# Experts' attention on one Trainium2 core: the transposes of the normalised average, the values' projection and the output's projection each placed one step later

## The reference, cut to what matters

```python
def expert_step(acc, params):
    qw, qb_, kw, kb_, vw, vb_, ow, ob_, g = params
    q = (x @ qw.T + qb_).reshape(B, S, H, Dh).transpose(0, 2, 1, 3)
    k = (x @ kw.T + kb_).reshape(B, S, H, Dh).transpose(0, 2, 1, 3)
    v = (x @ vw.T + vb_).reshape(B, S, H, Dh).transpose(0, 2, 1, 3)
    scores = jnp.einsum('bhqd,bhkd->bhqk', q, k) * scale
    p = jax.nn.softmax(scores, axis=-1)
    o = jnp.einsum('bhqk,bhkd->bhqd', p, v)
    o = o.transpose(0, 2, 1, 3).reshape(B, S, E) @ ow.T + ob_
    return (acc + o * g[..., None], None)
```

## Time and profile before

| | us |
|---|---|
| median of 3 runs | 2183.87 |
| lowest and highest of them | 2181.33, 2192.77 |
| the profiled execution, its own time | 2187.13 |
| its span, first to last instruction | 2185.3 |
| TensorE busy | 1855.6 |
| VectorE busy | 1673.8 |
| ScalarE busy | 1288.2 |
| GpSimd busy | 941.1 |

### The profile page before, as it was taken

The page is one execution under the profiler, slowest core; times in us unless marked ns, Lnnn a source line. Parts: engine busy times, 40 slices in busy tenths (PEclk is TensorE's granted clock), DMA queues, the critical chain, the costliest instruction groups (busy, mean ns, idle before and its releaser), DMA issues. The chain is left out here.

```text
span 2185.3 us, 50731 instructions
## 1 busy us (share of the span) xinstructions
PE 1855.6 (85%) x20464; PEld 954.8 (44%) x20464; DVE 1673.8 (77%) x2850; ACT 1288.2 (59%) x1848; POOL 941.1 (43%) x914
## 2 busy tenths in 40 slices
PE   5758999999999999999947898988888988988984
PEld 3542233233233333333223665665665655665663
DVE  3856777777777777777647978889878889879873
ACT  4423666666666666666725656666655656656652
POOL 0011111111111111111029958768768768768760
PEclk8956999999999999999968999999999999999998
DMA  1032223222323232323014333333333333333320
GB/s 36 1 76 50 49 57 58 50 55 55 64 60 65 60 64 60 64 60 61 2 39 119 89 95 103 100 96 107 95 96 103 100 95 103 100 96 102 95 69 15
DMA packets 101281, 156.36 MB, mean 72 GB/s; under 512 B 29335, under 2 KB 64185, under 8 KB 97209
## 3 DMA queue, kind: packets, MB, share of 16 engines
q1 hardware_dynamic: 98937, 152.19, 28.5%
q10 hardware_dynamic: 2112, 0.94, 0.3%
HBM read 98.03 MB, written 51.12 MB: 68 GB/s over the span
## 5 line engine op out<-in xcount | busy, mean ns | idle before, releaser
L824 DVE TENSOR_REDUCE ENM<-PM 128x1 f32<-128x512 f32 x1024 | 665.4, 687 | 212.3 <-PE PM L604 199.9
L735 ACT ACTIVATE EPT<-PA 128x1024 f32<-128x1024 f32 x512 | 514.6, 1021 | 214.7 <-PE PV L627 124.2
L604 PE MATMUL PM<-EKX,EQX 48*128 48x512 bf16 x1024 | 381.3, 393 | 18.9 <-DVE ENM L824 17.9
L1300 POOL TENSOR_TENSOR DRN<-DRN,DHALF 128x8 f32<-128x8 f32 x192 | 371.7, 1936 | 0.0
L524 POOL CAST ENMP<-ENM 128x16 bf16<-128x16 f32 x64 | 12.7, 198 | 748.0 <-DVE ENM L824 748.0
L627 PE MATMUL PV<-EPT,EVP 128*32 128x256 f32 x4096 | 327.9, 392 | 2.1 <-ACT EAVS L766 1.9
L1298 POOL TENSOR_TENSOR DQR<-DR 128x512 f32<-128x512 f32 x192 | 252.5, 1315 | 169.0 <-DVE DR L1581 169.0
L616 PE MATMUL PA<-EQX,EKX 51*128 51x512 bf16 x1024 | 254.6, 387 | 19.4 <-DMA EQX<-EROWS 15.4
L1344 PE MATMUL PM<-DWQKV,DXS 128*128 128x512 f32 x384 | 214.4, 641 | 26.9 <-ACT DRAW L1500 20.3
L604 PEld LDWEIGHTS PM<-EKX,EQX 48*128 48x128 bf16 x1024 | 93.8, 93 | 308.9 <-DVE ENM L824 222.0
L1500 ACT ACTIVATE DRAW<-PM 128x512 f32<-128x512 f32 x192 | 114.6, 597 | 169.5 <-DVE DR L1581 93.1
(11 more groups left out here) (207 smaller groups left out, 2858.2 us busy)
## 6 DMA issues: line engine op xcount, KB each, us to landing
DV<-d_vpark SPq DMA_DIRECT2D x192, 256.0 KB, 4.9
d_vpark<-DVT SPq DMA_DIRECT2D x48, 512.0 KB, 2.6
e_park<-EPARTS SPq DMA_DIRECT2D x64, 192.0 KB, 3.0
EQX<-e_park SPq DMA_DIRECT2D x32, 384.0 KB, 5.6
EKX<-e_park SPq DMA_DIRECT2D x32, 384.0 KB, 9.2
DWQKV<-in_WqkvR SPq DMA_DIRECT2D x6, 1536.0 KB, 10.0
e_park<-EPARTS SPq DMA_DIRECT2D x64, 128.0 KB, 2.7
e_park<-EPARTS SPq DMA_DIRECT2D x64, 64.0 KB, 2.1
```

The source lines that it names most:

```text
L604: pe.matmul(PM[:, r, :], lhsT=QX[64 * r:64 * r + KQ, b, hp, t * 128:(t + 1) * 128], rhs=KX[64 * r:64 * r + KQ, b, hp, :], start=True, stop ...
L735: s_.activation(PT[:, kt, pair * 2 * S:(pair + 1) * 2 * S], PA[:, 2 * pair:2 * pair + 2, :].rearrange("p a b -> p (a b)"), ACT.Exp, scale= ...
L824: v.tensor_reduce(NM[:, g % 2, t, j, 0:1], PM[:, r, :], AX.X, ALU.max, negate=True).then_inc(maxed, 1)
L1300: g.tensor_tensor(rn, rn, HALF[:, 0:8], ALU.pow).then_inc(rooted.sem, 1)
```

## The change

Three numbers in the table of uses and one on VectorE move. The values' projection goes from step 5 to step 6 (the seventh), the transposes of the normalised average from step 5 to step 6, the output's projection and the addition that reads it from step 6 to step 7 (the eighth). All engines take the step from `slot_uses`, ScalarE's `values_out` and `ont_out` included; the order of the uses of the bank PX stays what it was.

```diff
--- before.py
+++ after.py
@@ -359,9 +359,9 @@
     if not (first and g == 0):
         u += [(4, "avt")]
     if g % HG == 1 and more:
-        u += [(5, "v")]
+        u += [(6, "v")]
     if g % HG == 0 and not (first and g == 0):
-        u += [(5, "ont"), (6, "o")]
+        u += [(6, "ont"), (7, "o")]
     return u
 
 
@@ -869,7 +869,7 @@
                             normalise(gp, e * NG + (g - 1))
                         if s == 5 and g == 0:
                             v.tensor_copy(GC[:, :], GATE[:, :, bass.ds(e, 1)].rearrange("p n o -> p (n o)")).then_inc(gates, 1)
-                        if s == 6 and "o" in uses:
+                        if s == 7 and "o" in uses:
                             add_out(gp // HG, use(e, g, "o"))
 
                 chain = Chain(dve, q["step"])
```

## The result

The changed kernel takes 2204.59 us at the median of 10 runs (2195.32 to 2214.51), the kernel before 2182.79 us of 10 (2178.34 to 2192.77): a ratio of 1.0098, 95% interval 1.0075 to 1.0121, so 1% slower, some 22 us. The profiled execution took 2203.46 us, its span is 2201.6 us.

A forecast was written before the change was run, and what follows sets the result against it. TensorE, busy for 85% of the span, was taken as the bound, with gates set by the bringing in. Terms -1.0 - 1.1 + 2.4 + 6.0 = +6.3 us gave 2190.2 us, range 2179 to 2200.

The forecast's parts named there:

- The two waits: TensorE's waits for the normalised average, before its transposes and the values' projection: 29.4 us removed, only -1.0 us counting in full.
- What the gate waits for: First scores behind the values' slot: rows' DMAs land behind bringing in, which the change doesn't move; issuing them earlier brings nothing.
- `o`, `add_out` and the queues: Output's projection, its addition and DMA queues: 0 for `o` and `add_out`, at worst 0.5 us in last stretch; queues +2.4 us.
- EVW's load: SP's load waiting for `v`: goes out 8.6 us behind bringing in, may share engines with rows' packets; 0.4 us in six stretches.
- the six gates: Gates in stretches where SP also loads weights for queries, keys, output and values: holds growing from 0.9 to 2.9 us.
- the eight: The other gates of stretches 1 to 14: holds growing from 0.2 to 2.2 us.
- The clock: TensorE's clock behind the gates: longer holds bring 7 falls at 0.85 us each, +6.0 us.
- Every gate drops the clock: Slower rival: holds of 2.2 to 2.9 us at 14 gates each halve TensorE's clock; +14.3 us, 2198.2 us, chance 0.24.
- Holds only: Rival of no change: waits become holds one for one, neither clock nor load matters; 2181.8 us, chance 0.2.
- The gates move too: Faster rival: rows land earlier as they are issued earlier; 16 us gained, 2168 us, or 2154.5 us if unbound; chance 0.06.
- The gate at 954.59: Bringing in starts there, scores 13.2 us later against 12.1 us elsewhere; the one gate not holding, slack won -1.1 us.

The follow-up runs named there:

- the filled kernel: Changed kernel plus three unread 128x512 float32 projections on TensorE ahead of each of the 14 gates and the first stretch's; 2184.93 us, ratio 1.0003 to the kernel before.
- the new order of DMAs: Changed kernel with SP issuing the last of four bringing-in DMAs only after ScalarE issued the rows' four; 2158.61 us, ratio 0.9871; repeated on another chip 2163.80 us.

## Why the prediction was wrong

**Right.** *The two waits* went, all 30. *What the gate waits for*: the rows stayed behind the bringing in, the gates 11.4 to 13.1 us after its start; issuing the rows 1.1 us and more earlier gained nothing, and putting them ahead of the last 384 KB did. The rule of the Trainium skill's DMA: Bandwidth & Descriptors ("Queues, rings and completion order"), that an engine goes round its queues packet by packet, is not borne out in these runs: ScalarE's packets ran 10.7 us behind the start of bringing in, and 7.8 us behind it once SP's last DMA was held back. *`o`, `add_out` and the queues* cost nothing that can be seen; EVW's load went out 8.5 us behind the bringing in (forecast 8.6), and the 2.4 us set aside for it were not needed: the six gates concerned stand where they stood (0.1 us in their sum). In the last stretch the slot of the output gained 15.14 - 13.94 = 1.2 us (forecast 1.0), as it did in the others. The holds came out at 3.0 us on average at the six gates and 2.7 us at the eight, where 2.9 and 2.2 us were forecast.

**The step that failed** is the term *The clock*: 7 falls at 0.85 us, 6.0 us. Measured were 13 falls and 21.4 us, 1.6 us each. Both factors were too small. The number, because I drew a line between the longest harmless hold (1.05 us) and the one harmful hold (3.44 us), where the runs show falls at 32 of 36 holds of 1.19 us and more. The price, because a fall in the first stretch and one more in a slot of the output, both of 3.4 us, were all the trace of before had within the slots, and longer ones came: behind a gate 3.4 us cost about 1.05 us, as the row of the first gate had it (1.0), but 6.8 us cost 2.3 us and 17.1 us cost 5.9 us, and four of the 13 were of these. With 13 falls at 1.05 us the term would have been 13.7 us; the longer falls bring the other 7.7 us, and no bound of mine had them. The discount to 0.85 us had no row behind it, and the second row spoke against it: the fall at 949.80 made its slot of the output 18.40 us long instead of 16.85 us, 1.55 us.

**The rivals.** "Every gate drops the clock" was the right one, with its condition nearly met (13 of 14) and its price too low; it gave 2198 us. The rule of the Trainium skill's TensorE: Matmul & The Clock Gate ("HAM oscillation — how this bites in real kernels") is borne out in 13 of 14 stretches, with waits of 2.3 to 3.4 us; what it would cost, no row of before could say. "Holds only" is what the filled kernel shows: 2185 us, equal to before. "The gates move too" was wrong for the change as it stood: in the sum they came 2.0 us later.

*The gate at 954.59*, booked with -1.1 us, gained nothing: in its stretch the gate stands at 32.15 us behind the first exponential, as before (32.16). There bringing in went out at 19.5 instead of 19.0 us and the gate opened 12.7 us behind it, so the DMAs were as late as TensorE had been. TensorE had been late there because of the fall at 949.80. The prediction also says that one gate alone did not hold; of the 14 there were four (at 511.09, 852.90, 967.76 and 1024.34), and the other three opened 0.4 to 1.0 us later after the change, not earlier.

## What to carry to other kernels

A wait taken off an engine ahead of a transfer that already binds is not worth nothing; it can cost, because the idle time is gathered in one piece: here 32 of the 36 pieces of 1.19 to 3.39 us came with a fall of TensorE's clock to half, and none of the 20 up to 1.05 us. Before moving work, find the next gate and what sets its time, and free that first: here one small DMA put ahead of the last of four big ones turned a loss of 22 us into a gain of 25 to 28 us against the kernel before. And look at the whole program after adding instructions: of the five profiled kernels with unread matmuls ahead of the gates, four lost over 20 us in another stage.

## What was not expected of the hardware

- Falls of the clock can outlast the hold by far. Behind one hold of 3.08 us the clock stayed at 0.50 for 17.1 us, with TensorE busy for 16.55 of 16.90 us; behind others of the same length for 3.4 us. What decides was not found.
- Between no fall (holds up to 1.05 us, 20 gates) and falls at most gates (14 of 17 between 1.19 and 2.00 us) there is little room. It isn't a fixed point: with the new order of DMAs holds of 1.25 and 1.33 us had no fall, and one of 1.05 us had one.
- Float32 transposes in the hold kept the clock up about as well as matmuls: 12 of 14 gates without a fall. The Trainium skill's TensorE: Matmul & The Clock Gate, "Part 4: PE-mode transpose", has it that a transpose doesn't count as activity in the same way; here it did count.
- Two nearly empty matmul instructions a gate cost 22 us, most of it in a later stage, in gaps of up to 4.6 us that no wait of the profile accounts for. 47 gaps over 1.5 us, in 13 executions, end 1.2 to 1.9 us after a packet of the instruction queue is through.
